# Splitting the large position and one-hot operations of the edge binning into pieces of three tile pairs

## The chip, the cores and the metric

One NeuronCore of a Trainium2 chip runs the whole program. The metric is device time in microseconds of one execution; of the kernel before there are three timed runs, and one further execution was taken with the hardware profiler. The engines are called PE (TensorE, with its weight loads as PEld), DVE (VectorE), ACT (ScalarE), POOL (GpSimd) and SP (SyncE).

## What is computed

One layer of a graph network on N = 6250 nodes with 256 features. `xn` is the layer norm of `x`. Three things are added to `x`: the sum over 200000 weighted edges, a mixing term, and then an expert feed-forward block.

```python
xn = _layernorm(x)
msgs = values[:, None] * xn[col]                       # one message for each of 200000 edges
x = x + segment_sum(msgs, row, num_segments=6250) + mix(xn)
x = x + moe(_layernorm(x))
```

Only the edge sum is touched here. The edges come sorted by one of their two ends; the other end is random.

## The kernel before, in words

**Stages.** `norm_stage`, `mix_stage`, `edge_stage`, then routing and the experts (`ffn_stage`). The edges are cut into seven chunks (`NQ = 7`). The nodes make 49 blocks of 128 (`NB = 49`). For each chunk the edge stage walks over all 49 blocks; one such visit is a *step* (step 0 to 48 of a chunk), so there are 343 steps.

**What a step does in the edge stage.** The chunk has been *binned*: its edges have been sorted into the 49 blocks. In step t

- POOL issues three indirect DMAs that gather rows of `xn` into `G` (L1285). `G` has five buffers, and the gathers of step t wait for `stepped` of step t - 5.
- DVE makes one-hots for step t + 1 (L1440, L1445, in `one_hots`), adds the finished product of step t - 2 to the result (L1458, in `finish`, signals `summed`), and then does one share of the binning of the *next* chunk (`dve_share(q + 1, b)`, L1524). This order is written out in L1517 to L1526.
- ACT scales the one-hots by the edge weights (L1388) and copies a PE result (L1379).
- PE makes `edge_ap` (L1338), does its share of the binning of the next chunk (`pe_share`, L392), then waits for `summed` of step t - 2 (L1347) and for the gathers of step t (L1349), and makes six products into `edge_op` (the gathered ones at L1351, those of the windows at L1355). The last of them signals `stepped`.

**The binning.** `dve_share` has a table of step numbers. Steps 0 to 3 build the one-hots `onehot` of the chunk's edges by block (L426), steps 4 to 7 add them up pair by pair into running counts `before` (L445), steps 8 and 9 make offsets. Steps 10 to 13 (`SLOT_AT` to `HALF_AT`) run the lines that are changed: in steps 10 and 11 the base positions `start` are added to `before`, in steps 12 and 13 `before` is multiplied by `onehot`. The first half of the tile pairs (0 to 7) is done in steps 10 and 12 by one instruction of 7 x 686 = 4802 elements per partition; the second (7 to 15) in steps 11 and 13 by one of 8 x 686 = 5488 elements and one of 784 for pairs 15 and 16, which exist for four of the seven columns only. All are bf16, in place in `before`, and both inputs lie in SBUF (`start` is read with a broadcast). Only the last instruction of steps 11 and 13 signals a semaphore (`next_link`). From step 14 on, slots are read out of `before` (L499), and products and one-hots for PE are made (L511, L513).

**Where each chunk is binned.** Chunk 0 is binned in the mix stage, where `IN_SUMS` places its steps between units of other work (POOL gathers nothing there). Chunks 1 to 6 are binned in the edge stage during the products of the chunk in front of them. The products of the last chunk run beside the layer norm and the router scores of the nodes.

Of the kernel before, what the change touches and what calls it, by code (L numbers as in the profile page):

```python
# [31 lines left out]
KG, GN, DN = 4, 3, 3  # L32
CB = KG + DN
SC = GN + DN
NCH = NQ * CB
LP, SP2 = 17, 15
# [70 lines left out]
class Bins:  # L107
# [305 lines left out]
    def dve_share(self, dve, q, n):  # L413
# [9 lines left out]
        if self.HOT_AT <= n < self.CHAIN_AT:  # L423
            for k in range(2 * (n - self.HOT_AT), min(2 * (n - self.HOT_AT) + 2, CB)):
                w = REAL[k] // 2
# [16 lines left out]
        if self.CHAIN_AT <= n < self.BASE_AT:  # L442
            for t in range((n - self.CHAIN_AT) * self.LINKS_A_STEP, min((n - self.CHAIN_AT + 1) * self.LINKS_A_STEP, LP)):
                w = CB if t < SP2 else KG
# [34 lines left out]
        if self.SLOT_AT <= n < self.HALF_AT:  # L479
            late, part_ = divmod(n - self.SLOT_AT, 2)  # L480
            cut = SP2 // 2
            for a, b, w in ((0, cut, CB),) if part_ == 0 else ((cut, SP2, CB), (SP2, LP, KG)):
                piece = before[:, a:b, 0:w, :, :].rearrange("p t c b h -> p t (c b h)")
                if late == 0:
                    other, op = self.start[:, 0:w, :, :].rearrange("p (a c) b h -> p a (c b h)", a=1)\
                        .to_broadcast([P, b - a, w * NB * 2]), ALU.add
                else:
                    other, op = onehot[:, a:b, 0:w, :, :].rearrange("p t c b h -> p t (c b h)"), ALU.mult
                ins = nc.vector.tensor_tensor(piece, piece, other, op)
            if part_ == 1:  # L490
                self.next_link(dve, q, ins)
        s, late = divmod(n - self.HALF_AT, 2)
        if 0 <= s < self.HALVES:
            k, part_ = divmod(s, 2)
            a, b = self.half(k, part_)
            if late == 0:
                if part_ == 0:
                    w = LP if k < KG else SP2
# [19 lines left out]
        if n == self.MERGE_AT:  # L518
# [3 lines left out]
            near, row, w = self.dst_of[:, 0:KG, :], self.found[:, 0, :, :], self.found[:, 2, :, :]  # L522
# [7 lines left out]
        if n == self.MERGE_AT + 1:  # L530
            top, w, sign = self.bits[self.TOP][:, 0:KG, :], self.found[:, 2, :, :], self.sign_of[:, 0:KG, :]
# [28 lines left out]
        if n == self.UNPACK_AT:  # L560
            dve.wait_ge(self.kept, (q + 1) * CB)
            ids, top, rest = (x[:, KG:CB, :] for x in self.bits)
            w, sign = self.weight_of[:, KG:CB, :], self.sign_of[:, KG:CB, :]
# [1862 lines left out]
```

## Time and profile before

| | |
|---|---|
| three timed runs | 1991.59, 1996.81, 1999.81 us; median 1996.81 us |
| the profiled execution | 1989.69 us, its span 1988.0 us |
| mean granted TensorE clock | 0.956 |
| busy time in the span | PE 1764.5, PEld 1527.8, DVE 1380.9, ACT 1093.2, POOL 1286.6 us |
| gathers of the edge stage | 1029, the first at 271.2 us, the last at 1616.8 us |

The span runs from the first to the last instruction. Busy time is the time in which an engine executed something; waiting and issuing are not counted. A granted clock of 1.00 is 2.4 GHz, and the lower level, 0.50, is 1.2 GHz. In a row that names a wait, the time in brackets is how long the engine sat idle before the instruction, and what stands behind the arrow is what ended that idle time. "issue" means that nothing which the profile shows was waited for. Rows with "x6" merge that many instructions.

### The profile page before, as it was taken

The numbers are of one execution on the slowest core, as the hardware profiler recorded it, in microseconds if no ns is written. First come the engines' busy times: TensorE is split into PE (matmuls) and PEld (weight loads), VectorE is DVE, ScalarE is ACT, GpSimd is POOL, SyncE is SP. The second block draws the span as 40 slices with busy tenths as digits, with TensorE's granted clock in tenths as the row PEclk, the third lists the DMA queues.
The fourth block names the chain that finished last, engine by engine and source line by source line (L and its number), as shares of the span: only waits on it lengthen the run. The fifth ranks groups of instructions, "written<-read, shape, count | busy, mean of one in ns | idle before, by whom it ended". The sixth has DMA issues, their size and how long they took to land. (4 is left out here: it accounts for less than half of the span.)

```text
span 1988.0 us, 33518 instructions
## 1 busy us (share of the span) xinstructions
PE 1764.5 (89%) x10522; PEld 1527.8 (77%) x10522; DVE 1380.9 (69%) x2880; ACT 1093.2 (55%) x3267; POOL 1286.6 (65%) x1283
## 2 busy tenths in 40 slices
PE   5677878999899989998999999999999983999994
PEld 3366667988798889887988898889899972787773
DVE  6988458886888798788878986988677768010113
ACT  5632025556555655565556555655576652776662
POOL 1000367777777777777777777777777740777773
PEclk9988889999999999999999999999999986999997
DMA  7522453443233323332333333333344432344557
GB/s 255 196 87 95 138 173 122 139 131 117 91 107 104 112 91 106 105 112 90 105 105 108 93 107 104 104 99 104 106 133 133 136 109 70 102 144 131 164 161 228
DMA packets 130054, 244.30 MB, mean 123 GB/s; under 512 B 26533, under 2 KB 77620, under 8 KB 129880
## 3 DMA queue, kind: packets, MB, share of 16 engines
q0 software_dynamic: 59584, 161.78, 26.9%
q1 hardware_dynamic: 63852, 73.97, 11.4%
q10 hardware_dynamic: 6444, 6.40, 0.9%
q8 instruction: 89, 1.46, 0.3%
q14 instruction: 85, 0.70, 0.1%
HBM read 197.24 MB, written 45.77 MB: 122 GB/s over the span
## 5 line engine op out<-in xcount | busy, mean ns | idle before, releaser
L1285 POOL DMA_INDIRECT edge_G<-xn_scratch,edge_row_i x1029 | 1031.7, 1003 | 313.5 <-issue 290.6
L1388 ACT ACTIVATE edge_weighted<-edge_hots,bins_scale 128x128 f32<-128x128 bf16 x2058 | 638.5, 391 | 66.6 <-DVE edge_row_hots L1445 65.3
L1351 PE MATMUL edge_op<-edge_G,edge_weighted 128*128 128x256 f32 x2058 | 523.9, 391 | 62.1 <-DVE all_xn L1458 36.7
L1379 ACT COPY edge_A<-edge_ap 128x384 f32<-128x384 f32 x343 | 164.1, 478 | 533.1 <-PE edge_ap L1338 533.1
L1351 PEld LDWEIGHTS edge_op<-edge_G,edge_weighted 128*128 128x128 f32 x2058 | 366.7, 191 | 111.2 <-DVE all_xn L1458 50.7
L1440 DVE TENSOR_TENSOR edge_hots<-edge_numbers,bins_recb 128x768 bf16<-128x768 bf16 x343 | 190.6, 556 | 194.2 <-PE edge_ap L1338 190.0
L1338 PEld LDWEIGHTS edge_ap<-edge_weighted,edge_row_hots 128*128 128x128 f32 x2058 | 278.7, 192 | 39.1 <-issue 14.2
L1338 PE MATMUL edge_ap<-edge_weighted,edge_row_hots 128*128 128x128 f32 x2058 | 287.5, 276 | 11.6 <-ACT edge_weighted L1388 8.7
L1355 PE MATMUL edge_op<-bins_win,edge_A 128*128 128x256 f32 x1176 | 289.9, 383 | 0.0
L1355 PEld LDWEIGHTS edge_op<-bins_win,edge_A 128*128 128x128 f32 x1176 | 226.8, 193 | 31.9
L1355 PE MATMUL edge_op<-edge_win,edge_A 128*128 128x256 f32 x882 | 218.4, 384 | 0.0
L2320 DVE SCALAR_TENSOR_TENSOR exp_acc<-exp_ys,ffn_share,all_xn 128x256 f32<-128x256 f32 (+1 forms) x49 | 20.6, 481 | 248.9 <-DMA exp_ys<-ys_scratch 246.8
L1355 PEld LDWEIGHTS edge_op<-edge_win,edge_A 128*128 128x128 f32 x882 | 170.6, 193 | 24.2
L1445 DVE TENSOR_TENSOR edge_row_hots<-edge_numbers,bins_recd 128x384 f32<-128x384 f32 x343 | 187.8, 548 | 0.0
L1080 POOL TENSOR_TENSOR all_xn<-mix_xg,mix_qbias 128x1024 f32<-128x1024 f32 (+1 forms) x13 | 29.0, 2228 | 188.8 <-DVE mix_xg L1158 187.7
L392 PE MATMUL bins_bp<-bins_RH,bins_SL 128*128 128x147 bf16 x1582 | 142.0, 232 | 8.5 <-DVE bins_SL L513 8.0
L2184 POOL DMA_INDIRECT exp_xt<-hn_scratch,ffn_token x105 | 103.0, 981 | 71.6 <-POOLq L2007 40.0
L1458 DVE TENSOR_TENSOR all_xn<-all_xn,edge_op 128x256 f32<-128x256 f32 (+1 forms) x343 | 140.9, 411 | 9.0 <-PE edge_op L1355 8.8
L392 PEld LDWEIGHTS bins_bp<-bins_RH,bins_SL 128*128 128x128 bf16 x1582 | 122.4, 99 | 12.8 <-DVE bins_SL L513 7.5
L2190 POOL DMA_INDIRECT ys_scratch<-exp_yt,ffn_target x105 | 108.0, 1028 | 32.3 <-issue 28.3
L2239 PE MATMUL exp_dn<-ffn_w2s,exp_gT 128*128 x420 | 120.1, 409 | 0.0
L2226 PE MATMUL exp_up<-exp_xT,exp_w1x 128*128 128x128 f32 x840 | 113.6, 279 | 0.1
(343 smaller groups left out, 2080.2 us busy)
## 6 DMA issues: line engine op xcount, KB each, us to landing
edge_G<-xn_scratch,edge_row_i POOLq DMA_INDIRECT x1029
exp_ys<-ys_scratch SPq DMA_DIRECT2D x12, 1024.0 KB, 6.4
ln_xin<-in_x SPq DMA_DIRECT2D x12, 512.0 KB, 5.3
xn_scratch<-ln_xnb ACTq DMA_DIRECT2D x12, 512.0 KB, 6.3
xnT_scratch<-ln_xT SPq DMA_DIRECT2D x12, 512.0 KB, 6.8
mix_xg<-xn_scratch SPq DMA_DIRECT2D x12, 512.0 KB, 3.8
mix_ek<-xnT_scratch SPq DMA_DIRECT2D x12, 512.0 KB, 4.7
mix_xg<-in_x SPq DMA_DIRECT2D x12, 512.0 KB, 3.9
```

The lines of the kernel that those rows point to most:

```text
L392: last = nc.tensor.matmul(self.bp[:, 0:self.NV * NB], self.SL[:, s % 2, t - a, :, side], self.R[:, s % 2, t - a, :, :, side].rearrange("p ...
L1285: pool.indirect_dma_start(out=G[:, t % AHEAD, i, :], out_offset=None, in_=xn_dram, in_offset=bass.IndirectOffsetOnAxis(ap=row_i[:, q % 2, ...
L1338: last = nc.tensor.matmul(ap[j][:, i * P:(i + 1) * P], row_hots[:, j, i, :], weighted[:, j, GN + i, :], start=True, stop=True)
L1351: nc.tensor.matmul(op[j][:, :], weighted[:, j, i, :], G[:, rb, i, :], start=i == 0, stop=False)
L1355: last = nc.tensor.matmul(op[j][:, :], A[:, j, i, :], win[q % 2][:, i, :], start=False, stop=i == DN - 1)
L1379: nc.scalar.copy(A[:, j, :, :].rearrange("p c s -> p (c s)"), ap[j][:, :]).then_inc(a_kept, 1)
L1388: last = nc.scalar.activation(weighted[:, t % 2, i, :], hots[:, t % 2, i // 2, :, i % 2], ACT.Copy, scale=scale[:, b, i:i + 1])
L1440: nc.vector.tensor_tensor(hots[:, t % 2, :, :, :], bins.slots_of[:, :, :].rearrange("p (a s) h -> p a s h", a=1).to_broadcast([P, NE // 2, ...
L1445: nc.vector.tensor_tensor(row_hots[:, t % 2, :, :], rows_of_window[:, :].rearrange("p (a s) -> p a s", a=1).to_broadcast([P, DN, P]), recd ...
L1458: nc.vector.tensor_tensor(h[:r, b, :], h[:r, b, :], op[(q * NB + b) % 2][:r, :], ALU.add).then_inc(summed, 1)
L2226: last = nc.tensor.matmul(up[t % 2][f][:, :], w1x[:, t % WB, k, f * P:(f + 1) * P], xT[:, t % 2, k, :], start=k == 0, stop=k == KC - 1)
L2239: last = nc.tensor.matmul(dn[t % 2][:, :], gT[:, t % DOWN, f, :], w, start=False, stop=f == KC - 1)
```

## The change

The one instruction for pairs 0 to 7 becomes three, of 3, 3 and 1 pairs; the one for pairs 7 to 15 becomes three, of 3, 3 and 2 pairs; the one for pairs 15 to 17 stays. This holds for the additions and for the products, in all seven chunks. Elements, order, buffers and semaphores stay as they are; the last piece carries the signal.

```diff
         if self.SLOT_AT <= n < self.HALF_AT:
             late, part_ = divmod(n - self.SLOT_AT, 2)
             cut = SP2 // 2
-            for a, b, w in ((0, cut, CB),) if part_ == 0 else ((cut, SP2, CB), (SP2, LP, KG)):
+            parts = ((0, cut, CB),) if part_ == 0 else ((cut, SP2, CB), (SP2, LP, KG))
+            for a, b, w in ((x, min(x + 3, end), w) for first, end, w in parts for x in range(first, end, 3)):
                 piece = before[:, a:b, 0:w, :, :].rearrange("p t c b h -> p t (c b h)")
                 if late == 0:
                     other, op = self.start[:, 0:w, :, :].rearrange("p (a c) b h -> p a (c b h)", a=1)\
                         .to_broadcast([P, b - a, w * NB * 2]), ALU.add
                 else:
                     other, op = onehot[:, a:b, 0:w, :, :].rearrange("p t c b h -> p t (c b h)"), ALU.mult
                 ins = nc.vector.tensor_tensor(piece, piece, other, op)
             if part_ == 1:
                 self.next_link(dve, q, ins)
```

## Rows read from the trace of the kernel before

**Rows 1.** Waits over the whole span: who waited for what, total us, times, longest us.

```profile
POOL edge_G L1285 <- issue: 290.6, 954, 0.3
...
POOL edge_G L1285 <- PE edge_op L1355: 20.7, 68, 0.3
...
PE edge_op L1351 <- DMA edge_G<-xn_scratch,edge_row_i: 25.2, 14, 3.2
```

**Rows 2.** Timeline of POOL while chunk 6 is binned: start us, us, instruction, idle before.

```profile
1281.95 3.15 POOL L1285 DMA_INDIRECT edge_G<-xn_scratch,edge_row_i  x1 [0.30 <-issue]
...
1286.66 2.63 POOL L1285 DMA_INDIRECT edge_G<-xn_scratch,edge_row_i  x1 [0.30 <-issue]
...
1290.84 2.88 POOL L1285 DMA_INDIRECT edge_G<-xn_scratch,edge_row_i  x1 [0.30 <-issue]
1294.03 0.94 POOL L1285 DMA_INDIRECT edge_G<-xn_scratch,edge_row_i  x1 [0.30 <-issue]
1295.27 2.63 POOL L1285 DMA_INDIRECT edge_G<-xn_scratch,edge_row_i  x1 [0.30 <-issue]
```

**Rows 3.** Timeline of DVE, same stretch (the second row merges 5488 and 784 elements).

```profile
1290.25 2.65 DVE L489 TENSOR_TENSOR bins_BH<-bins_BH,bins_onehot 128x4802 bf16<-128x4802 bf16 x1
...
1294.08 3.49 DVE L489 TENSOR_TENSOR bins_BH<-bins_BH,bins_onehot 128x5488 bf16<-128x5488 bf16 x2
```

**Rows 4.** Groups of DVE instructions by line and shape: busy us, mean ns, idle before.

```profile
L489 DVE TENSOR_TENSOR bins_BH<-bins_BH,bins_onehot 128x5488 bf16<-128x5488 bf16 x7 | 21.1, 3011 | 0.0
...
L489 DVE TENSOR_TENSOR bins_BH<-bins_BH,bins_onehot 128x784 bf16<-128x784 bf16 x7 | 3.9, 559 | 0.0
```

**Rows 5.** Windows, steps 10 to 14 of chunk 6's binning: stretch, us, busy by engine, clock.

```profile
1281.60:1303.60 22.00, 16.18 (x83) 13.91 (x82) 21.80 (x27) 11.17 (x35) 18.34 (x13) 1.00 0.22 66
```

**Rows 6.** Timeline of PE: step 13 beside chunk 6's binning; step 15 beside each chunk's.

```profile
1295.79 1.53 PE L1351 MATMUL edge_op<-edge_G,edge_weighted 128*128 128x256 f32 x6 [1.88 <-DMA edge_G<-xn_scratch,edge_row_i]
...
340.47 1.53 PE L1351 MATMUL edge_op<-edge_G,edge_weighted 128*128 128x256 f32 x6 [0.22 <-DMA edge_G<-xn_scratch,edge_row_i]
...
534.69 1.46 PE L1351 MATMUL edge_op<-edge_G,edge_weighted 128*128 128x256 f32 x6
...
726.21 1.56 PE L1351 MATMUL edge_op<-edge_G,edge_weighted 128*128 128x256 f32 x6 [0.43 <-DVE all_xn L1458]
...
920.50 1.46 PE L1351 MATMUL edge_op<-edge_G,edge_weighted 128*128 128x256 f32 x6
...
1112.05 1.53 PE L1351 MATMUL edge_op<-edge_G,edge_weighted 128*128 128x256 f32 x6 [0.38 <-DVE all_xn L1458]
...
1304.97 1.53 PE L1351 MATMUL edge_op<-edge_G,edge_weighted 128*128 128x256 f32 x6 [0.51 <-DMA edge_G<-xn_scratch,edge_row_i]
```

**Rows 7.** Timeline of DVE: the addition that each step 15 of group 6 needs.

```profile
337.58 0.41 DVE L1458 TENSOR_TENSOR all_xn<-all_xn,edge_op 128x256 f32<-128x256 f32 x1
...
531.73 0.41 DVE L1458 TENSOR_TENSOR all_xn<-all_xn,edge_op 128x256 f32<-128x256 f32 x1
...
725.74 0.41 DVE L1458 TENSOR_TENSOR all_xn<-all_xn,edge_op 128x256 f32<-128x256 f32 x1
...
917.31 0.41 DVE L1458 TENSOR_TENSOR all_xn<-all_xn,edge_op 128x256 f32<-128x256 f32 x1
...
1111.51 0.41 DVE L1458 TENSOR_TENSOR all_xn<-all_xn,edge_op 128x256 f32<-128x256 f32 x1
...
1303.21 0.41 DVE L1458 TENSOR_TENSOR all_xn<-all_xn,edge_op 128x256 f32<-128x256 f32 x1
```

**Rows 8.** Timeline of PE in the mix stage, where chunk 0 is binned.

```profile
130.59 1.29 PE L392 MATMUL bins_bp<-bins_RH,bins_SL 128*128 128x147 bf16 x9 [7.31 <-DVE bins_SL L513]
```

**Rows 9.** Windows at two lower clocks: stretch, us, busy by engine, granted clock.

```profile
528.00:534.00 6.00, 4.33 (x12) 3.57 (x13) 5.83 (x10) 1.86 (x7) 4.71 (x5) 0.72 0.37 109
1208.00:1214.00 6.00, 5.20 (x21) 4.37 (x22) 4.46 (x9) 2.02 (x7) 4.56 (x5) 0.72 0.34 102
```

## The prediction

> **What bounds the kernel now.** I went from the waits to the timelines. In the waits, POOL's gathers never sat idle for more than 0.3 us, 954 times for nothing the profile shows and 68 times for PE [rows 1]: from 271 to 1617 us POOL issues without a pause. One would think that POOL sets the pace. But PE waited for a gather only 14 times, 25.2 us in all [rows 1]; mostly it reaches a step later than the step's data. So the question is where those few waits lie.
>
> They lie beside the changed instructions. A gather normally takes 0.94 us; the one that starts while DVE runs a large operation takes 2.6 to 3.2 us [rows 2]. Its end shows why: the gather from 1290.84 ends at 1293.72, and the 4802-element product ran from 1290.25 to 1292.90 [rows 2, 3], so it ends 0.82 us behind DVE's instruction. It is held until that instruction is over and then does the rest of its work. Each of the four large operations of a chunk holds one gather; the four are longer than 0.94 by 2.21 + 1.69 + 1.94 + 1.69 = 7.5 us [rows 2]. After them PE waits 1.88 us for data in step 13 [rows 6].
>
> In the same steps there is a second limit. From 1281.6 to 1303.6 DVE is busy 21.80 of 22 us [rows 5], and PE needs its addition before each step. Where PE waits for a gather there, DVE is right behind.
>
> **The change, part by part.**
>
> *DVE's cost.* Seven chunks times four large operations, each with two more instructions: 56. The elements stay. From 5488 and 784 elements, 3011 and 559 ns [rows 4], an element costs (3011 - 559)/4704 = 0.521 ns, and 559 - 784 x 0.521 = 150 ns is left as the fixed part of one instruction. Not all of that delays the next: the 784 elements add 3.49 - 3.01 = 0.48 us to the merged stretch [rows 3, 4], and their elements alone are 0.41. So one more instruction right behind another of its kind costs 0.07 us. The ends are 0 (the elements cannot get fewer) and 0.150; I take 0.07, because it is measured on this very pair. That is 8 x 0.07 = 0.56 us for a chunk.
>
> The Trainium skill, "VectorE: DVE Perf Modes", section "The TRN2 errata — SBUF-src ops pay a fixed extra latency per instruction", speaks against the change: one large tile pays the fixed part once, many small tiles pay it each, and the measured fixed part is about 150 cycles, at 0.96 GHz an estimated 0.156 us. By it the 56 instructions would cost 8.7 us. The trace agrees with that length for one instruction alone, but not for one behind another.
>
> *POOL's gain.* Pieces of three pairs are 2058 elements: about 1.22 us long, starting 1.14 us apart (1.07 + 0.07). Does a held gather get through between two pieces? The pair of 5488 and 784 elements is the row to read: the second follows at once and also has both inputs in SBUF. The gather from 1295.27 ends at 1297.90 [rows 2]; the first instruction ended at 1297.09, the second at 1297.57 [rows 3, 4]. It ended 0.81 us behind the first, as where nothing of the kind follows. So it passes between them. A gather that starts 0.59 us into a 4802-element product would be held until 1.22 and not 2.65 us; one that starts 1.19 us into the 5488 elements until 2.36 and not 3.01. Over the four: 1.43 + 0.65 + 1.43 + 0.65, about 4.1 of the 7.5 us; a second short hold in a last piece may take a few tenths back.
>
> *What that is worth.* Where the gather no longer comes last, DVE's addition does. So I read, for step 15 beside each of the six chunks binned in the edge stage, how far PE's start lies behind the end of that addition [rows 6, 7]: 340.47 - 337.99 = 2.48, 534.69 - 532.14 = 2.55, 0.06, 2.78, 0.13 and 1.35 us. The 0.06 is the handover. What can be won is 2.42, 2.49, 0, 2.72, 0.07 and 1.29, together 9.0 us. The 4.1 us of POOL are more than the largest of these, so the gathers are no longer last, and the rest of the 4.1 only lengthens POOL's lead. Of the gain, two chunks hold a clock loss: beside chunk 2, from 528 to 534 us the mean granted clock was 0.72, which is 6 x 0.28/0.5 = 3.4 us at 1.2 instead of 2.4 GHz and 1.7 us of PE lost [rows 9], after PE's long waits for gathers; that of chunk 4 is like it. With shorter waits I expect it to go. If both stay, 3.4 us of the 9.0 do.
>
> *What is paid for it.* DVE is the limit in these steps, so its 0.56 us count in full in each of the six chunks, 3.4 us, and also in the two where nothing can be won. In the mix stage PE waited 7.31 us for DVE's first half [rows 8]; POOL gathers nothing there, and 0.56 us are pure loss. Together 3.9 us.
>
> *Sum.* 9.0 won, 3.9 paid: 5.1 us less. The profiled execution took 1989.69 us, 0.4% below the median of the runs; 1984.6 there is 1991.7 us against 1996.81. That is 0.26%. About 0.5% (10 us) is what a measurement of this kernel can tell from no change.
>
> The ends: at 0 per instruction 9.0 us are won; at 0.150 they cost 8.4 and 0.6 us is left; with the two clock losses staying, the time would be 2.8 us longer at that end.
>
> **The rivals.**
>
> *The pieces cost their full fixed part*, 0.150 us each: 0.6 us less, 1996.2 us. For it: the single length. Against it: the 0.48 us of the pair.
>
> *The gather does not pass between pieces.* A run of equal pieces in place might hold it to the end of the run. Then POOL is held as now and 0.14 us longer each time, PE waits as before, and DVE's 3.9 us come on top: slower, 2000.7 us. It decides if gathers still end 0.8 us behind the last piece. Against it stands the pair, where the second instruction is small, though.
>
> *DVE waits in its turn.* If the gather that got through keeps the next piece from starting until it is done, every operation pays up to 0.82 us: 24 operations beside gathers are 19.7 us, with 3.9 paid and 9.0 won 14.6 us slower, 2011.4 us. It decides from 0.21 us per operation on (5.1/24). Against it: the 784 elements took 559 ns on the mean [rows 4] with a gather just let through. The Trainium skill, "SBUF — State Buffer", section "Who interferes with whom", would have it so: whichever starts first gets the shared pair for the whole instruction and the other is blocked. The trace bears that out for DVE first; for a gather first it shows nothing like it.
>
> *POOL does set the pace.* If its 4.1 us of each of six chunks all came off the end, that would be 24.6 us less, 0.6 paid in the mix stage: 1972.8 us. For it: POOL never pauses [rows 1]. Against it: DVE's 21.80 of 22 us [rows 5], and two chunks of six where step 15 starts 0.06 and 0.13 us behind DVE [rows 6, 7].
>
> *The clock elsewhere.* Late in most chunks PE runs at the lower level for about 3.4 us, as from 1208 us on [rows 9], in a stretch that the change does not touch. One such more or fewer is 1.7 us; that widens the range by a few us, and gets no case of its own.
>
> **How the numbers follow.** Forecast 0.64, full fixed part 0.14, no passing 0.08, DVE blocked 0.05, POOL's pace 0.09. The first three lie within 0.5%. A few hundredths of the forecast reach 10 us by its lower end and luck with the clock: faster 0.12 with POOL's pace; slower 0.06 with DVE blocked; the same 0.82. The range takes 9.0 us below the median and 4 above (no passing), plus the scatter of a median of runs that lie 8 us apart: 1983 to 2001. POOL's pace and DVE blocked stay outside.
>
> **What would show it.** Right: line 489 has 2058-element instructions of about 1.22 us, and no gather beside them is longer than some 2.3 us; PE's waits for gathers fall from 25.2 us to a few; in steps 11 to 15 PE's wait ends with DVE's addition in all six chunks, and DVE is as busy as before. Wrong: gathers of 2.6 us and more, a DVE that idles between pieces, or steps 13 to 15 shorter than DVE's work in them.

## The result, and the profile after

The changed kernel takes **1980.9 us** (median of four runs, 1980.03 to 1981.11). The kernel before, run beside it, takes 1997.26 us (four runs, 1991.59 to 1999.81). The ratio is 0.9921 (95% interval 0.99 to 0.9943), so the change is worth 16.4 us, 0.8%. The forecast was 1991.7 us, the range 1983 to 2001: the direction was right, the size was not, and the time lies 2.1 us below the range. The profiled execution took 1981.11 us (span 1979.4), where that of before took 1989.69: from profile to profile it is 8.6 us.

PE's waits for DVE's additions in the kernel before, and then the waits of the changed kernel, over the whole span, columns as in [rows 1]:

```profile
PE edge_op L1351 <- DVE all_xn L1458: 36.7, 44, 1.9
```

```profile
POOL edge_G L1286 <- issue: 287.8, 944, 0.3
...
PE edge_op L1352 <- DVE all_xn L1459: 54.2, 54, 1.9
POOL edge_G L1286 <- PE edge_op L1356: 28.9, 78, 3.2
...
PE edge_op L1352 <- DMA edge_G<-xn_scratch,edge_row_i: 3.1, 2, 2.9
```

PE's waits for gathers fall from 25.2 us in 14 places [rows 1] to 3.1 us in 2, neither of them in steps 11 to 15: 2.92 us stand at the first step of the edge stage, 0.16 in a step 6. DVE's additions take their place, 54.2 us where 36.7 were. POOL now pauses too, up to 3.2 us: it is so far ahead that all five gather buffers are full and it waits for PE to free one.

POOL while chunk 6 is binned (additions up to 1280.5 us, products behind them), to hold against [rows 2]:

```profile
1273.69 1.31 POOL L1286 DMA_INDIRECT edge_G<-xn_scratch,edge_row_i  x1 [0.30 <-issue]
1275.30 1.26 POOL L1286 DMA_INDIRECT edge_G<-xn_scratch,edge_row_i  x1 [0.30 <-issue]
1276.87 0.94 POOL L1286 DMA_INDIRECT edge_G<-xn_scratch,edge_row_i  x1 [0.30 <-issue]
1278.12 1.99 POOL L1286 DMA_INDIRECT edge_G<-xn_scratch,edge_row_i  x1 [0.30 <-issue]
...
1284.20 1.26 POOL L1286 DMA_INDIRECT edge_G<-xn_scratch,edge_row_i  x1 [0.30 <-issue]
...
1287.01 1.98 POOL L1286 DMA_INDIRECT edge_G<-xn_scratch,edge_row_i  x1 [0.30 <-issue]
```

The same stretch on DVE, to hold against [rows 3]; the changed line is now L490, and a row merges the pieces of one step:

```profile
1272.95 2.80 DVE L490 TENSOR_TENSOR bins_BH<-bins_BH,bins_start 128x2058 bf16<-128x2058 bf16 x3
...
1276.59 0.41 DVE L1459 TENSOR_TENSOR all_xn<-all_xn,edge_op 128x256 f32<-128x256 f32 x1
1276.92 3.62 DVE L490 TENSOR_TENSOR bins_BH<-bins_BH,bins_start 128x2058 bf16<-128x2058 bf16 x4
```

And the pieces as a group, to hold against [rows 4]:

```profile
L490 DVE TENSOR_TENSOR bins_BH<-bins_BH,bins_start 128x2058 bf16<-128x2058 bf16 x28 | 33.2, 1226 | 0.2
```

No gather takes longer than 1.99 us, where four took 2.6 to 3.2. The one from 1278.12 ends at 1280.11. The second piece of the row at 1276.92 started at 1278.06 and was over 1.22 us later, at 1279.28: the gather ended 0.83 us behind one piece, with two more pieces still to run. So gathers pass between pieces. The row of three pieces takes 2.80 us against 2.65 for the whole operation, the row of four 3.62 against 3.49: 0.13 to 0.15 us for two more instructions.

PE's steps 11 to 15 in the same stretch, to hold against [rows 6]:

```profile
1277.06 1.56 PE L1352 MATMUL edge_op<-edge_G,edge_weighted 128*128 128x256 f32 x6 [1.23 <-DVE all_xn L1459]
1281.98 1.56 PE L1352 MATMUL edge_op<-edge_G,edge_weighted 128*128 128x256 f32 x6 [1.40 <-DVE all_xn L1459]
1285.95 1.56 PE L1352 MATMUL edge_op<-edge_G,edge_weighted 128*128 128x256 f32 x6 [0.44 <-DVE all_xn L1459]
1290.87 1.56 PE L1352 MATMUL edge_op<-edge_G,edge_weighted 128*128 128x256 f32 x6 [1.40 <-DVE all_xn L1459]
1295.55 1.56 PE L1352 MATMUL edge_op<-edge_G,edge_weighted 128*128 128x256 f32 x6 [1.15 <-DVE all_xn L1459]
```

Every wait ends with DVE: the addition from 1276.59 is over at 1277.00, and PE starts at 1277.06. So it is in all six chunks. DVE is as full as in [rows 5]:

```profile
1276.60:1298.60 22.00, 17.15 (x88) 14.84 (x89) 21.83 (x36) 11.13 (x34) 17.16 (x16) 1.00 0.32 92
```

**Where the 8.6 us lie.** From PE's timeline I take the start of each step's first product and add up pass times over the six chunks of the edge stage (the pass of step n runs from the start of step n - 1 to that of step n). The first product of the edge stage starts at 278.53 us before and at 280.45 after; from there to the first product of the last step it is 1344.55 and 1334.56 us. Of these 10.0 us, steps 11 to 15 give 5.3 (144.03 to 138.72 us), step 40 gives 3.4 and step 36 gives 1.1; the rest, 0.2, is spread over the other steps. Ahead of the edge stage 1.9 us are lost, and behind it some 0.5 won: 10.0 - 1.9 + 0.5 = 8.6.

Step 40 is a matter of the clock. Beside chunk 1, the windows (columns as in [rows 5]) and PE's steps 39 and 40, first of before:

```profile
437.20:443.20 6.00, 5.95 (x28) 5.10 (x29) 4.40 (x9) 2.43 (x10) 4.64 (x5) 0.72 0.36 106
```

```profile
437.25 2.32 PE L1351 MATMUL edge_op<-edge_G,edge_weighted 128*128 128x256 f32 x6 [1.86 <-DVE all_xn L1458]
442.86 1.50 PE L1351 MATMUL edge_op<-edge_G,edge_weighted 128*128 128x256 f32 x6
```

and then of the changed kernel:

```profile
437.20:443.20 6.00, 5.91 (x36) 5.36 (x37) 6.00 (x13) 4.00 (x14) 4.60 (x5) 1.00 0.38 115
```

```profile
437.29 1.56 PE L1352 MATMUL edge_op<-edge_G,edge_weighted 128*128 128x256 f32 x6 [1.86 <-DVE all_xn L1459]
441.20 1.50 PE L1352 MATMUL edge_op<-edge_G,edge_weighted 128*128 128x256 f32 x6
```

The same work behind the same wait takes 5.61 us at a mean granted clock of 0.72 (a stretch at 1.2 GHz) and 3.91 us at 1.00 (2.4 GHz). Before, five of the six chunks had such a slow step 40; after, three.

### The profile page after: what moved, and what is told of

Same layout as the page of the kernel before. It is cut to its first block and busy times, and to the rows that moved or that the text cites. A ratio compares the mean times of both kernels' runs of the same rounds, so it can differ in the third digit from the quotient of the medians.

```text
span 1979.4 us, 33574 instructions
## 1 busy us (share of the span) xinstructions
PE 1760.7 (89%) x10522; PEld 1524.9 (77%) x10522; DVE 1382.9 (70%) x2936; ACT 1094.5 (55%) x3267; POOL 1267.4 (64%) x1283
## 5 line engine op out<-in xcount | busy, mean ns | idle before, releaser
L1286 POOL DMA_INDIRECT edge_G<-xn_scratch,edge_row_i x1029 | 1012.5, 984 | 318.8 <-issue 287.8
L1352 PE MATMUL edge_op<-edge_G,edge_weighted 128*128 128x256 f32 x2058 | 522.0, 390 | 58.0 <-DVE all_xn L1459 54.2
L1339 PE MATMUL edge_ap<-edge_weighted,edge_row_hots 128*128 128x128 f32 x2058 | 287.4, 276 | 11.5 <-ACT edge_weighted L1389 8.7
L1356 PEld LDWEIGHTS edge_op<-edge_win,edge_A 128*128 128x128 f32 x882 | 169.8, 193 | 23.8
```

What stands on the lines that cost most here:

```text
L1286: pool.indirect_dma_start(out=G[:, t % AHEAD, i, :], out_offset=None, in_=xn_dram, in_offset=bass.IndirectOffsetOnAxis(ap=row_i[:, q % 2, ...
L1339: last = nc.tensor.matmul(ap[j][:, i * P:(i + 1) * P], row_hots[:, j, i, :], weighted[:, j, GN + i, :], start=True, stop=True)
L1352: nc.tensor.matmul(op[j][:, :], weighted[:, j, i, :], G[:, rb, i, :], start=i == 0, stop=False)
L1356: last = nc.tensor.matmul(op[j][:, :], A[:, j, i, :], win[q % 2][:, i, :], start=False, stop=i == DN - 1)
```

## The experiments

The kernels stand in three groups, each run on one chip with the kernel before beside it: before_again to chunk0_whole (median of before there 1991.45 us), after_again to spread (1999.72) and the last two (1994.02). Their profiles in one table, by the sums just described ("low" counts the stretches at 1.2 GHz that begin in the edge stage):

| | median us | ratio to before | edge stage us | steps 11–15 | step 40 | low | PE's waits for gathers, us / times |
|---|---|---|---|---|---|---|---|
| before, first profile | 1997.26 | | 1344.55 | 144.03 | 31.92 | 7 | 25.2 / 14 |
| before_again | 1992.64 | 1.0001 | 1346.48 | 146.63 | 31.94 | 8 | 28.1 / 15 |
| before_third | 1994.23 | 0.9996 | 1350.74 | 152.39 | 30.24 | 11 | 30.5 / 14 |
| changed | 1980.9 | 0.9921 | 1334.56 | 138.72 | 28.56 | 3 | 3.1 / 2 |
| after_again | 1982.06 | 0.9913 | 1333.15 | 137.78 | 26.87 | 2 | 4.9 / 3 |
| pieces_1 | 1988.81 | 0.9986 | 1341.18 | 146.15 | 26.87 | 2 | 3.7 / 4 |
| pieces_4 | 1983.05 | 0.9952 | 1337.48 | 137.68 | 30.23 | 4 | 15.1 / 12 |
| chunk0_whole | 1979.93 | 0.9933 | 1333.19 | 138.51 | 26.88 | 2 | 4.7 / 3 |
| start_psum | 1979.91 | 0.9909 | 1333.30 | 138.43 | 26.88 | 2 | 3.1 / 1 |
| fewer_buffers | 1981.02 | 0.9913 | 1332.89 | 138.07 | 26.87 | 2 | 5.1 / 3 |
| spread | 1959.36 | 0.9803 | 1316.22 | 112.96 | 23.51 | 4 | 13.1 / 21 |
| spread_small | 1954.0 | 0.9788 | 1312.56 | 112.69 | 31.92 | 5 | 7.4 / 9 |

**before_again**: the kernel before, unchanged, 11 runs.

> The kernel before, unchanged, for a second profile and more times. Theory A (the gain is the waits for held gathers, and with them stretches at the lower clock whose number varies): the time lies between 1990 and 2000 us and the runs differ among themselves by several us; PE waits for gathers 20 to 30 us in all beside the steps 12 to 15; the edge stage holds seven or more low-clock stretches of 3.4 us, each worth about 1.7 us, and their number explains how this profile differs from the first. Theory B (the runs of before differ somewhere else): the edge stage is as long as in the first profile, and the difference lies in the experts or the start.

Measured: 1992.64 us (1990.28 to 1994.09), ratio 1.0001 (0.9992 to 1.001). What follows: the 7 us between the first profile and the 1997 us beside it do not appear here; this profile (1991.21 us) has 2.6 us more in steps 11 to 15 than the first one, and its edge stage is 1.9 us longer. Within the edge stage, the two profiles differ mainly in these steps.

**pieces_1**: pieces of one pair, 17 to a chunk and kind in place of 7.

```diff
-            ... (x, min(x + 3, end), w) for first, end, w in parts for x in range(first, end, 3)):
+            ... (x, min(x + 1, end), w) for first, end, w in parts for x in range(first, end, 1)):
```

> Pieces of one pair: 18 more instructions for a chunk than the changed kernel. Theory A (DVE sets the time of steps 10 to 15): 18 x 0.07 = 1.3 us for a chunk, seven chunks 8.8 us slower than the changed kernel's 1980.9, so about 1990; steps 11 to 15 still end with DVE's addition. Rival (POOL sets the pace): gathers are held 0.5 us at most, POOL saves some 2.5 us more for a chunk, 15 us faster, about 1966.

Measured: 1988.81 us, ratio 0.9986 (0.9977 to 0.9996). There are 20 more instructions to a chunk than in the changed kernel, not the 18 of the expectation. Beside all chunks but the first, steps 11 to 14 take 4.84 to 4.92, 5.34, 4.24 and 5.34 us, each some 0.07 to 0.08 us longer for each further instruction. POOL waits 77.0 us for free buffers, in 157 places, where the changed kernel's waits 28.9: all the lead it could want, and the kernel is slower. What follows: the price of an instruction right behind another is 0.07 us, and POOL does not set the pace.

**pieces_4**: the same line with 4 for 3.

> Pieces of at most four pairs: 4 and 3, 4 and 4; four instructions fewer for a chunk than the changed kernel. Theory A: 4 x 0.07 x 7 = 2.0 us faster than 1980.9, about 1979, and the gathers, held up to 1.6 us, still come in time. Rival (POOL sets the pace): each gather is held up to 0.4 us longer, up to 10 us slower, about 1990.

Measured: 1983.05 us, ratio 0.9952 (0.9938 to 0.9965), where the count of instructions alone had made it about 1979. The expectation was missed. The nearest kernel on its chip is chunk0_whole, which leaves chunk 0 whole as well: 0.9933 (0.992 to 0.9947), so the two intervals overlap a little. The gathers that the longer pieces hold, on POOL beside chunk 6, and PE's waits:

```profile
1279.06 2.34 POOL L1286 DMA_INDIRECT edge_G<-xn_scratch,edge_row_i  x1 [0.30 <-issue]
```

```profile
PE edge_op L1352 <- DMA edge_G<-xn_scratch,edge_row_i: 15.1, 12, 3.0
```

Summed over the gathers that run beside the changed instructions of a chunk, they are longer than 0.94 us by 4.9 to 5.6 us, where the changed kernel has 3.1 to 3.5; and gathers come last again beside chunks 1, 4 and 6. But in this profile these waits are not what makes the kernel longer: steps 11 to 15 take 137.68 us in all, no more than the changed kernel's 138.72, since the saved instructions outweigh the waits. The time is lost in step 40 (30.23 us, and 26.88 in chunk0_whole) and step 36 (25.83 and 24.73), which the edit does not touch. What follows: smaller pieces are paid in instructions and larger ones bring back waits, but that three pairs are better than four in the steps at issue is not shown.

**chunk0_whole**: no split where no gather can be held, in chunk 0.

```diff
+            size = LP if q == 0 else 3
-            ... (x, min(x + 3, end), w) for first, end, w in parts for x in range(first, end, 3)):
+            ... (x, min(x + size, end), w) for first, end, w in parts for x in range(first, end, size)):
```

> The change without chunk 0, which is binned in the mix stage where POOL gathers nothing. Theory A: 0.6 us faster than the changed kernel by DVE's eight instructions, and one low-clock stretch less at 130 us may make it 1.1 to 1.7 us: 1979.2 to 1980.3; the edge stage as in the changed kernel. Rival (the split helps the mix stage too): slower than 1980.9.

Measured: 1979.93 us (1976.72 to 1981.15), ratio 0.9933 (0.992 to 0.9947). It is about 1 us below the changed kernel's first runs, which lie at 1980.03 to 1981.11 and were not taken beside it; that is within the scatter, so the 0.56 us in the mix stage are neither shown nor refuted by these times. Nor does the profile settle it: PE's first half of chunk 0 starts 23.87 us after the first product of the binning, as in the changed kernel (23.88; before 23.32), but from 107 to 113 us the mean granted clock is 0.72 here and 1.00 there. The 0.56 us stand in PE's row below (on the mix stage, in the next section).

**after_again**: the changed kernel, unchanged, on the chip where before is slowest.

> The changed kernel, unchanged, so that it and the kernel before are timed on the same chip. Theory A: about 1980 to 1982 us against some 1991 to 1992 of the kernel before there, that is 0.994 to 0.995; low-clock stretches of the edge stage three or so, none beside steps 12 to 15. Rival (the first measured ratio of 0.992 holds): 1976 or 16 us faster than before.

Measured: 1982.06 us (1977.94 to 1983.5), ratio 0.9913 (0.9897 to 0.9929). The expected 0.994 to 0.995 was missed: on this chip the gain is as large as in the first measurement. What follows: of the two kernels it is the one before that moves more from measurement to measurement (medians 1991.45 to 1999.72); the two medians of the changed one are 1980.9 and 1982.06.

**start_psum**: whole operations as before, but the base positions are copied to PSUM first, so that the additions have one input in SBUF only. The products keep both.

```diff
+            self.next_link(dve, q, nc.vector.tensor_single_scalar(
+                self.bp[:, 0:CB * NB].bitcast(I32), self.start[:, :, :, :].rearrange("p c b h -> p (c b h)").bitcast(I32),
+                0, op=ALU.bitwise_or))
...
-                    other, op = self.start[:, 0:w, :, :].rearrange("p (a c) b h -> p a (c b h)", a=1)\
+                    other, op = self.bp[:, 0:CB * NB].bitcast(BF16)[:, 0:w * NB * 2].rearrange("p (a e) -> p a e", a=1)\
```

> The kernel before with whole operations, but the base positions are copied to PSUM (one more instruction of about 0.45 us for a chunk), so that the additions have one input in SBUF; the products keep two. Theory A (a gather is held by an instruction with both inputs in SBUF): gathers beside the additions of steps 10 and 11 take 0.95 us, those beside the products of steps 12 and 13 still 2.6 to 2.9; some 3.9 of 7.5 us are freed for a chunk, PE's waits for gathers fall to a third or less, time 1981 to 1986. Rival (any long DVE instruction holds a gather): gathers of 2.6 to 3.2 us beside the additions too, and 0.45 x 7 = 3 us slower than before, about 1995.

Measured: 1979.91 us, ratio 0.9909 (0.9895 to 0.9923), a little under the expected range. POOL beside chunk 6, and DVE in the same stretch:

```profile
1273.71 0.95 POOL L1288 DMA_INDIRECT edge_G<-xn_scratch,edge_row_i  x1 [0.30 <-issue]
1274.96 0.95 POOL L1288 DMA_INDIRECT edge_G<-xn_scratch,edge_row_i  x1 [0.30 <-issue]
...
1277.46 0.95 POOL L1288 DMA_INDIRECT edge_G<-xn_scratch,edge_row_i  x1 [0.30 <-issue]
1278.71 0.95 POOL L1288 DMA_INDIRECT edge_G<-xn_scratch,edge_row_i  x1 [0.30 <-issue]
...
1282.47 3.21 POOL L1288 DMA_INDIRECT edge_G<-xn_scratch,edge_row_i  x1 [0.30 <-issue]
```

```profile
1273.59 2.66 DVE L492 TENSOR_TENSOR bins_BH<-bins_BH,bins_bp 128x4802 bf16<-128x4802 bf16 x1
...
1277.42 3.48 DVE L492 TENSOR_TENSOR bins_BH<-bins_BH,bins_bp 128x5488 bf16<-128x5488 bf16 x2
...
1282.20 2.65 DVE L492 TENSOR_TENSOR bins_BH<-bins_BH,bins_onehot 128x4802 bf16<-128x4802 bf16 x1
```

Beside the additions (1273.59 to 1276.25 and 1277.42 to 1280.90) every gather takes 0.95 us. Beside the product at 1282.20, just as long but with both inputs in SBUF, one takes 3.21. What follows: it is the second SBUF input that holds a gather, not DVE's being busy. The Trainium skill, "SBUF — State Buffer", section "Who interferes with whom", says that an instruction of VectorE with at most one SBUF input, outside the modes that use two ports for one tensor, does not contend with GpSimd, and that one with two SBUF inputs contends with a GpSimd instruction that reads SBUF; these rows agree, 0.95 us against 3.21. And two of the four holds may stay (3.0 to 4.0 us a chunk): POOL's lead covers them, and PE waits 3.1 us in one place, at the first step of the stage.

**fewer_buffers**: the changed kernel with four gather buffers in place of five (`AHEAD` 5 to 4, L1172).

> The changed kernel with four gather buffers in place of five. Theory A (what keeps PE from waiting in steps 12 to 15 is the lead that POOL has built up by step 10): the lead is cut by about one step, 3.8 us, where it is largest (steps 40 to 44), so about 3 us are left at step 10 as in the kernel before; gathers come last again in some of steps 12 to 15, PE waits 5 to 15 us in all, 3 to 8 us slower than the changed kernel. Rival (only the length of the hold counts): as the changed kernel within 2 us.

Measured: 1981.02 us, ratio 0.9913 (0.9899 to 0.9926); POOL's lead (from the end of the last gather of step 10 to PE's first product of that step) is only 2.8 to 2.9 us, where it is 2.8 to 6.6 in the changed kernel and 2.4 to 5.8 in the first profile of the one before; PE waits 5.1 us in 3 places. Expected was a loss; there is none. What follows: with the gathers held 3.1 us a chunk (3.7 beside the first), a lead of 2.9 us is enough. What the change brings is the shorter hold, not the longer lead.

**spread**: the theory's last step was that DVE's work in steps 11 to 15 is what remains. So here the additions (pieces of two pairs) are spread over steps 10 to 13, and each of the seven columns of products is done by itself, in two halves, in the step before the one that reads it.

```diff
+            parts = (((0, 3, CB),), ((3, 8, CB),), ((8, 13, CB),), ((13, SP2, CB), (SP2, LP, KG)))[n - self.SLOT_AT]
...
+        k, at = divmod(n - (self.HALF_AT - 1), 4)
+        if 0 <= k < CB and at == 0:
+            w = LP if k < KG else SP2
+            for a, b in ((0, w // 2), (w // 2, w)):
+                piece = before[:, a:b, k, :, :].rearrange("p t b h -> p t (b h)")
...
```

> The same work arranged differently: the additions in pieces of two pairs over steps 10 to 13, and the products by columns, two halves for each, in the step in front of the one that reads the column, where DVE has idle time. Theory A (after the change DVE's work in steps 10 to 15 is the limit, 23.2 us for five steps against about 17 to 18 that PE needs): the five steps shorten to 19 or 20 us, the gathers stay ahead because no DVE instruction is longer than 0.9 us; 3 us for each of six chunks, 15 to 20 us faster than the changed kernel, about 1963. Rival (POOL's own 3.75 us for a step is the limit after all): the lead falls to 2 us and PE waits for gathers, no more than 5 us faster.

Measured: 1959.36 us, ratio 0.9803 (0.979 to 0.9817). Steps 11 to 15 fall from 138.72 to 112.96 us, and their waits are for gathers again. PE beside chunk 6:

```profile
1264.81 1.53 PE L1355 MATMUL edge_op<-edge_G,edge_weighted 128*128 128x256 f32 x6 [0.50 <-DMA edge_G<-xn_scratch,edge_row_i]
1268.70 1.53 PE L1355 MATMUL edge_op<-edge_G,edge_weighted 128*128 128x256 f32 x6 [0.40 <-DMA edge_G<-xn_scratch,edge_row_i]
```

Part of the gain goes back: steps 36 and 38, where the last columns' products now lie, take 5.11 and 5.89 us (the changed kernel's take 4.15 and 4.86). What follows: after the change DVE did bound these steps, and POOL is next: 112.96 us are 3.77 for a step, and three gathers at 0.95 + 0.30 us are 3.75.

**before_third**: the kernel before once more, on a third chip.

> The kernel before once more, for a profile on another chip: there it took 1991.5 us on one chip and 1999.7 on another, the changed kernel 1980.9 and 1982.1. Theory A (what differs is how much PE waits for held gathers and how often the clock falls, and both are sensitive to small differences where the gathers come last): if the time is near 2000 us, the profile shows more passes in which gathers come last in steps 12 to 15 than four of six, or more than eight low-clock stretches in the edge stage; the stage is longer by most of the difference. Rival (such a chip is slower elsewhere): the edge stage lasts 1344 to 1347 us again and the rest is longer.

Measured: 1994.23 us (1990.18 to 1996.92), ratio 0.9996 (0.9986 to 1.0005). This profile is 6.0 us longer than the first, and its edge stage 6.2. PE beside chunks 1 and 2, two steps 13 of it:

```profile
335.24 1.53 PE L1351 MATMUL edge_op<-edge_G,edge_weighted 128*128 128x256 f32 x6 [3.81 <-DMA edge_G<-xn_scratch,edge_row_i]
...
529.31 2.90 PE L1351 MATMUL edge_op<-edge_G,edge_weighted 128*128 128x256 f32 x6 [3.72 <-DMA edge_G<-xn_scratch,edge_row_i]
```

These two passes take 7.31 and 7.15 us, where DVE's work needs 3.83 (the six matmuls of the second row took 2.90 us and not 1.53, at the lower clock); gathers come last beside all six chunks, and steps 11 to 15 take 8.4 us more than in the first profile (1.7 come back in step 40). What follows: this profile is longer through held gathers and the low clock behind them. How much they cost goes with POOL's lead at step 10. Over the 18 chunks in the three profiles of the kernel before, steps 11 to 15 take 22.5 to 22.6 us where the lead is 5.4 us or more, 23.8 to 25.3 where it is 3.3 to 4.5, and 24.8 to 27.9 where it is 2.9 or less. In the two profiles of the changed kernel they take 22.3 to 23.2 us at any lead from 2.8 to 6.6.

**spread_small**: spread with smaller pieces, to hold gathers less (additions of one pair, columns in thirds), and with the products of the last two columns at steps 26 and 30, where DVE has room.

```diff
-            for a, b, w in ((x, min(x + 2, end), w) for first, end, w in parts for x in range(first, end, 2)):
+            for a, b, w in ((x, x + 1, w) for first, end, w in parts for x in range(first, end)):
...
+        at = [self.HALF_AT - 1 + 4 * k for k in range(5)] + [26, 30]
...
-            for a, b in ((0, w // 2), (w // 2, w)):
+            for a, b in ((0, 6), (6, 11), (11, w)):
```

> The spread kernel with smaller pieces: additions of one pair, products by columns in thirds, and the last two columns earlier, out of the busy steps 33 to 38. Theory A (in the spread kernel DVE no longer limits steps 10 to 15, and POOL's pace of 3.75 us a step plus its holds does): gathers are held some 1 to 1.5 us less for a chunk, the chunk shortens from 188 to about 187 us, and PE waits less than 13 us for gathers; steps 36 and 38 return from 5.1 and 5.9 us to 4.2 and 4.9; together 5 to 9 us faster than 1959. Rival (DVE is the limit again, with some 20 more instructions for a chunk): 1.4 us for each chunk, 8 us slower.

Measured: 1954.0 us (1948.91 to 1955.57), ratio 0.9788 (0.9775 to 0.9802), the lowest of all, though its interval overlaps that of spread: 40 us below the kernel before on its chip. PE's waits for gathers fall from 13.1 us to

```profile
PE edge_op L1356 <- DMA edge_G<-xn_scratch,edge_row_i: 7.4, 9, 2.7
```

and steps 36 and 38 are back at 4.1 to 4.4 and 4.86 to 5.02 us. Five of its six steps 40 are slow, 31.92 us against the 23.51 of spread, where none is: 8.4 us that it has by luck of the clock against it. What follows: against spread it wins 11.5 us in steps 36 and 38 and only 0.3 in steps 11 to 15. The moved columns pay, the smaller pieces hardly.

## Why the prediction was wrong in size, point by point

**DVE's price: right.** 0.07 us for an instruction right behind another: the merged rows give 0.13 to 0.15 us for two, the steps 0.14 each (step 12 goes from 4.79 to 4.93 us), pieces_1 some 0.07 to 0.08 for one. The full 0.150, the rival at 1996.2 us, is refuted.

**A gather passes between pieces: right**, as the row from 1278.12 shows; the rival at 2000.7 us falls. What the gathers beside the changed instructions take beyond 0.94 us falls from 6.6 to 7.5 us a chunk to 3.1 to 3.5, by 4.1 on the mean, as was forecast.

**DVE does not wait in its turn: right.** A piece that is kept waiting would be longer, or start later: the mean of 28 is 1226 ns where 1.22 us was forecast, and the merged rows are 0.13 to 0.15 us longer than before and no more. The rival at 2011.4 us falls. A gather that starts first shows the same: the one from 1276.87 us starts 0.05 us before the piece at 1276.92, it takes 0.94 us and the piece 1.22, and neither is held. So the rule of the Trainium skill that was cited beside this rival (its section words it for the modes that use two ports for one tensor, and counts two SBUF inputs among what contends) does not hold here for a gather that comes first.

**POOL does not set the pace: right** by pieces_1 and fewer_buffers; the rival at 1972.8 us falls.

**Steps 11 to 15: right, for the profile it was read from.** Won 9.0 and paid 3.4, so 5.6 us less, was the forecast; 5.3 was measured. It holds chunk by chunk: less the 0.56 us paid, the forecast was 1.86, 1.93, -0.56, 2.16, -0.49 and 0.73 us, and 1.70, 2.01, -0.65, 2.16, -0.56 and 0.65 were measured. The two clock losses beside chunks 2 and 4 went with the waits, as expected.

**The mix stage: the part named was right, the rest not foreseen.** PE's first half of chunk 0 in the changed kernel, to hold against [rows 8]:

```profile
131.72 1.29 PE L392 MATMUL bins_bp<-bins_RH,bins_SL 128*128 128x147 bf16 x9 [7.87 <-DVE bins_SL L514]
```

7.87 against 7.31 us is the 0.56 that was forecast. Another 0.57 us stood there already at the first product of the binning (107.84 us against 107.27), ahead of any changed line, and 0.79 came behind it up to 280.45 us; there more time passes at the low clock (the mean granted clock from 134 to 282 us is 0.85, where it was 0.87).

**The step that failed** is the last of the sum: "1984.6 there is 1991.7 us against 1996.81". Of the 10.8 us between the forecast and the result it makes 7.1. It carried the 5.1 us over to the median as if the 7.1 us by which the runs lie above that profile were work the change leaves alone. The runs of the changed kernel do not have them: its profiled execution took 1981.11 us and its median is 1980.9. The profile of before was a quick one, below all its timed runs. Three profiles of the kernel before have 144.0, 146.6 and 152.4 us in steps 11 to 15; what differs between them is how long PE waits for held gathers, and the low clock behind such waits. In these steps the change does not take off a fixed amount: it brings them close to DVE's own time, 138.7 and 137.8 us in its two profiles, wherever POOL's lead stood. Held against before_third it takes off 13.7 us there, not 5.3. The prediction even read this for two chunks of six, where nothing could be won, and did not ask how often the other state of those chunks would come. Carried out as a level and not as a difference, the sum gives 1984.6 us for the changed kernel; 1980.9 was measured.

**The rest, 3.7 us, is mostly the term "the clock elsewhere"**, which was given no case of its own. It measured 3.4 us in step 40 of the first pair and 5.1 between before and after_again (31.92 to 26.87). That it belongs to the change in part is likely, since the three profiles of before have 14 slow steps 40 of 18 and the two of the changed kernel 5 of 12. But steps 38 and 39 take the same 4.86 and 5.87 to 5.94 us in the first profiles of both kernels, so neither a hold nor a wait in or just ahead of it decides: the two rows shown above start their step 39 at 437.25 and 437.29 us behind the same wait of 1.86 us, and one is followed by a slow pass, the other by a quick one. spread_small shows that an edit can also move it the wrong way. Why it falls as it does stays open, and how much of the 3.4 us is luck with it. So does step 36, 1.1 us shorter, which nothing in the sum had.

One thing is argued and not shown: that the 1999.72 us of before on the second chip, and the first medians of 1997, come from the same waits. No execution that slow was profiled; before_third, at 1995.71, is the nearest.

## What to carry to other kernels

When a change takes away a wait, forecast the level that the next limit sets (here DVE's work in five steps) and not the difference to one profile, and take two or three profiles of the kernel before, since a wait that depends on when two engines meet differs from one execution to the next. A large two-input operation of DVE beside GpSimd's gathers can be cut so that a piece is about as long as the gather's own pace (here 1.23 us against 0.95 + 0.30): of the sizes tried, pieces of one pair made steps 11 to 15 longer (146.15 us), and four pairs did no worse there than three (137.68 against 138.72). Or give it one operand in PSUM. Once the wait is gone, spread the work of the engine that bounds the next: spread is 22.7 us below after_again on the same chip, more than the split itself brought.

## What was unexpected of the hardware

The addition with one operand in PSUM ran as fast as that with both in SBUF: 2.66 us for 4802 bf16 elements in start_psum against 2.65 for the product of the same size [rows 3], and it held no gather.

The kernel before moves between chips, with medians of 1991.45, 1999.72 and 1994.02 us, while the changed one has 1980.9 and 1982.06 in its two measurements. On one chip it does not scatter less: 1977.94 to 1983.5 us in five runs of after_again, where the kernel before beside it lies at 1996.45 to 2001.99.

A step of the same instructions behind the same wait takes 5.60 us or 3.92 us, by the granted clock alone, in step 40 of all kernels here but spread, which has only quick ones; none of the edits was made to control it, and between the profiles it is worth up to 8.4 us (31.92 against 23.51).
